# A four-layer transformer on one core: norms of keys and queries as products that accumulate into the feature banks

## The reference, cut to what matters

```python
def _apply_kernel(x, orf):                      # orf: 64 x 16
    m, d_k = orf.shape
    proj = jnp.einsum('bhld,md->bhlm', x, orf) / d_k ** 0.25
    norm = jnp.sum(x * x, axis=-1, keepdims=True) / (2.0 * math.sqrt(d_k))
    return (jnp.exp(proj - norm) + EPS) / math.sqrt(m)
...
q_phi, k_phi = _apply_kernel(q, orf), _apply_kernel(k, orf)
kv = jnp.einsum('bhlm,bhld->bhmd', k_phi, v)
ksum = jnp.sum(k_phi, axis=2)
num = jnp.einsum('bhlm,bhmd->bhld', q_phi, kv)
den = jnp.einsum('bhlm,bhm->bhl', q_phi, ksum)
out = num / den[..., None]
```

## Time and profile before

| | |
|---|---|
| median of 3 runs | 4754.18 us (4749.86 to 4757.36) |
| the profiled execution, its own time | 4758.76 us |
| its span, first to last instruction | 4757.0 us |
| mean granted TensorE clock over the span | 0.954 of full |
| PE busy | 4457.9 us (94%) |
| DVE / ACT / POOL busy | 3497.9 / 2808.7 / 1012.3 us |
| first product of the FFN that follows the first attention | at 795.4 us |

### The profile page before, as it was taken

The page is one execution under the profiler, slowest core; times in us unless marked ns, Lnnn a source line. Parts: engine busy times, 40 slices in busy tenths (PEclk is TensorE's granted clock), DMA queues, the critical chain, the costliest instruction groups (busy, mean ns, idle before and its releaser), DMA issues.

```text
span 4757.0 us, 66155 instructions
## 1 busy us (share of the span) xinstructions
PE 4457.9 (94%) x25753; PEld 1669.5 (35%) x25756; DVE 3497.9 (74%) x3850; ACT 2808.7 (59%) x5305; POOL 1012.3 (21%) x990
## 2 busy tenths in 40 slices
PE   8888888999997999999999999999999999999886
PEld 5444444666662222222222222222222232222285
DVE  3443447887887778888777888777888988888432
ACT  3222232333333778888777777777777757787721
POOL 2333335344422110000211111112111011100213
PEclk9888889999997999999999999999999999999998
DMA  3001000012212421211333221223222221222232
GB/s 103 25 29 58 19 19 11 10 49 77 71 71 67 128 79 67 69 48 62 121 97 106 73 76 68 83 95 122 71 80 75 63 70 45 87 67 79 72 116 54
DMA packets 230533, 330.73 MB, mean 70 GB/s; under 512 B 37030, under 2 KB 171752, under 8 KB 228168
## 3 DMA queue, kind: packets, MB, share of 16 engines
q1 hardware_dynamic: 227340, 318.63, 20.3%
q0 software_dynamic: 2880, 7.87, 0.8%
HBM read 218.95 MB, written 98.04 MB: 67 GB/s over the span
## 4 chain that ended last, share of the span: by engine, by line
PE 69%; DVE 10%; DMA 3%; POOL 2%; issue 2%; ACT 1%; SPq 1%; POOLq 0%; DVEq 0%; another core or an unknown queue 0%; ACTq 0%
PE ps L751 68%; DVE mx L1630 4%; PE ps L754 2%; DMA pk<-Ob 1%; DVE stat L1454 1%; DVE hn L1448 1%; DVE hn L1609 0%; DMA rd<-pk 0%; DVE hn L1604 0%; SPq L2117 0%; DMA KS<-kd 0%; DVE eb L1465 0%; DMA QS<-mrow 0%; ACT Pb L1376 0%; DVE hs L1440 0%
## 5 line engine op out<-in xcount | busy, mean ns | idle before, releaser
L1630 DVE TENSOR_REDUCE mx<-ps 128x1 f32<-128x1024 f32 x2048 | 2407.3, 1219 | 449.9 <-PE ps L751 446.7
L1376 ACT ACTIVATE Pb<-ps 128x512 f32<-128x512 f32 x4096 | 2202.6, 597 | 533.1 <-PE ps L751 529.0
L751 PE MATMUL ps<-QS,KS 98*128 98x512 bf16 x4096 | 1255.4, 387 | 16.5 <-ACT Pb L1376 7.7
L751 PE MATMUL ps<-Pb,VA 128*32 128x512 f32 x8192 | 1105.0, 612 | 0.1
L751 PE MATMUL ps<-KM,QM 64*128 64x512 bf16 x4096 | 661.1, 390 | 47.3 <-DVE mx L1630 45.7
L751 PEld LDWEIGHTS ps<-QS,KS 98*128 98x128 bf16 x4096 | 260.1, 98 | 1100.1 <-ACT Pb L1376 908.3
L751 PEld LDWEIGHTS ps<-KM,QM 64*128 64x128 bf16 x4096 | 179.3, 93 | 605.1 <-issue 357.0
L751 PEld LDWEIGHTS ps<-Pb,VA 128*32 128x32 f32 x8192 | 161.8, 108 | 403.2 <-issue 402.2
L1944 POOL CAST mrow<-mres 16x128 bf16<-16x128 f32 x64 | 18.1, 283 | 1293.2 <-ACT mres L1198 1293.2
L1502 DVE TENSOR_TENSOR phi<-ps,ns 128x1024 f32<-128x1024 f32 x64 | 78.2, 1222 | 188.6 <-PE ps L751 188.4
L751 PE MATMUL ps<-wdT,hT 128*128 128x256 f32 (+1 forms) x768 | 194.3, 396 | 15.5 <-DVE X L1615 14.1
(11 more groups left out here) (255 smaller groups left out, 4500.9 us busy)
## 6 DMA issues: line engine op xcount, KB each, us to landing
QM<-qd SPq DMA_DIRECT2D x128, 256.0 KB
KM<-kd SPq DMA_DIRECT2D x128, 256.0 KB
qd<-parts SPq DMA_DIRECT2D x96, 256.0 KB, 2.7
kd<-parts SPq DMA_DIRECT2D x96, 256.0 KB, 2.8
QS<-qd SPq DMA_DIRECT2D x64, 384.0 KB
KS<-kd SPq DMA_DIRECT2D x64, 384.0 KB
vdr<-vst SPq DMA_DIRECT2D x64, 256.0 KB, 2.5
den<-rd SPq DMA_DIRECT2D x64, 256.0 KB
```

The costliest lines, as they stand in the source:

```text
L751: return eng.matmul(out, a, b, start=start, stop=stop, skip_group_check=skip)
L1376: eng.activation(Pb[(u - 1) % 9], o, ACT.Exp, bias=0.0, scale=0.25).then_inc(act_A, 1)
L1630: eng.tensor_reduce(mx4[qc % 2][:, 4 * i + q, h:h + 1], o, AX, ALU.max).then_inc(dve_D, 1)
```

## The change

The norms are no longer a result of their own. A block matrix `Nblk` (128 x 512, laid out as `Wblk` is, each block filled with -0.125) is loaded, and the squares `k2` and `q2` are multiplied with it on the same row tiles as `kT` and `qT` are with `Wblk`, accumulating into the same banks. ACT takes the exponential of the keys from the banks (before: DVE added, ACT worked from `phi`). The steps `kn` and `nq`, DVE's addition and its four splitting instructions, `n8`, `nq`, `selq` and their transfers and POOL's conversion go. The plan's rules are rewritten in smaller pieces: `o` and `q` steps are split, and key steps stand between most query steps.

```diff
 def keys_order(b):
-    made = lambda C: [("k", C, 0), ("k", C, 1), ("v", C, 0), ("v", C, 1), ("kn", C)]
+    made = lambda C: [("k", C, 0), ("k", C, 1), ("v", C, 0), ("v", C, 1)]
...
 def queries_order(b, chunks, way):
...
-        for ht in range(2):
-            yield [("q", C, ht)]
-        yield [("fq", C), ("nq", C)]
-        for ht in range(2):
-            for g in range(2):
-                yield [("pq", C, ht, g)]
-            yield [("num", C, ht)] + ([("res", C)] if ht else [("ap0", stats)] if stats is not None else [])
+        yield [("q", C, 0)]
+        yield [("q", C, 1), ("fq", C)]
+        for ht, g in ((0, 0), (0, 1), (1, 0)):
+            yield [("pq", C, ht, g)]
+        yield [("num", C, 0)] + ([("ap0", stats)] if stats is not None else [])
+        yield [("pq", C, 1, 1)]
+        yield [("num", C, 1), ("res", C)]
...
-    behind = {"q": (0, 2), "nq": (2,), "pq": (0, 1, 0, 1), "num": (0, 2), "o": (0, 1)}
+    behind = {"q": (1, 2), "pq": (1, 1, 1, 2), "num": (0, 3), "o": (1, 0)}
...
         def phi_(n):
             w.wait_ge(act_k, at["k", C, 1])
+            w.wait_ge(pool_k2, at["k", C, 1])
             w.wait_ge(dve_setup, 4)
+            w.wait_ge(ld_n, 16)
             if n:
-                w.wait_ge(dve_phi, n)
+                w.wait_ge(act_phi, n)
             for ht in range(2):
-                for r in range(2):
-                    s = slice(64 * r, 64 * r + 64)
-                    d = mm(bank(1 + r)[:, 256 * ht:256 * ht + 256], kT[C % 2][s, ht, j * P:(j + 1) * P], Wblk[s, 256 * r:256 * r + 256])
+                for x, wt_ in ((kT, Wblk), (k2, Nblk)):
+                    for r in range(2):
+                        s = slice(64 * r, 64 * r + 64)
+                        d = mm(bank(1 + r)[:, 256 * ht:256 * ht + 256], x[C % 2][s, ht, j * P:(j + 1) * P], wt_[s, 256 * r:256 * r + 256],
+                               x is kT, x is k2)
...
         def pq(C, ht, g):
+            w.wait_ge(pool_q, at["q", C, 1])
             for k in range(2):
                 s, c = slice(32 * (2 * g + k), 32 * (2 * g + k) + 32), slice(P * (2 * g + k), P * (2 * g + k) + P)
                 mm(bank(b5 + k), Wblk[s, c], qT[i][s, ht, :], True, False)
-            w.wait_ge(dve_nq, 3 * at["nq", C])
-            w.wait_ge(pool_setup, 6)
             for k in range(2):
-                d = mm(bank(b5 + k), selq[0:96, 4 * ht + 2 * g + k, :], way_of(C)["stk"][0:96, :], False, True)
+                s, c = slice(32 * (2 * g + k), 32 * (2 * g + k) + 32), slice(P * (2 * g + k), P * (2 * g + k) + P)
+                d = mm(bank(b5 + k), Nblk[s, c], way_of(C)["q2"][s, ht, :], False, True)
...
         def phi_(n):
-            w.wait_ge(dve_phi, n + 1)
-            eng.activation(phi[n % 3], phi[n % 3], ACT.Exp, bias=0.0, scale=1.0).then_inc(act_phi, 1)
+            w.wait_ge(pe_phi, n + 1)
+            if n > 2:
+                w.wait_ge(pe_kv, n - 2)
+            eng.activation(phi[n % 3], bank(1, 2), ACT.Exp, bias=0.0, scale=1.0).then_inc(act_phi, 1)
...
-            w.wait_ge(ld_selq, 16)
-            eng.tensor_copy(flat(selq[0:96]), flat(phq[0][0:96, 0:2, :])).then_inc(pool_setup, 1)
...
-            load(n8, t["n8"]).then_inc(ld_n, 16)
-            load(flat(nq), t["nq"]).then_inc(ld_n, 16)
+            load(Nblk, t["nb"]).then_inc(ld_n, 16)
...
-            load(flat(phq[0][0:96, 0:2, :]), t["selq"]).then_inc(ld_selq, 16)
```

More of the change, by code:

```diff
@@ L49, in keys_order @@
             n = 4 * C + j
-            yield [("phi", n)] + [("kv", n - 2)] * (n % 16 > 1)
+            yield [("phi", n)]
+            if n % 16 > 1:
+                yield [("kv", n - 2)]
             if ahead:
-                yield ahead[j:j + 1] if j < 3 else ahead[3:]
+                yield ahead[j:j + 1]
         if b == 0:
@@ L516, in program @@
     Wblk = take("Wblk", [P, 512])
-    n8 = take("n8", [P, 8])
-    nq = take("nq", [P, 2, 96])
-    selq = take("selq", [P, 8, P], BF16)
+    Nblk = take("Nblk", [P, 512])
     kvS = take("kvS", [P, 256])
@@ L527, in program @@
     va = [take(f"va{i}", [P, 4, 16, 32]) for i in range(2)]
-    ns = [take(f"ns{i}", [P, 4, 16]) for i in range(2)]
     phi = [take(f"phi{i}", [P, 1024]) for i in range(3)]
@@ L760, in k @@
             if C < 4:
[L761 to L764, removed]
+                if C:
+                    w.wait_ge(act_k, at["k", C - 1, ht])
             elif ht:
@@ L866, in q @@
             else:
-                w.wait_ge(act_kn, 4)
+                w.wait_ge(act_k, at["k", 3, 1])
             mm(bank(b4), WT["q"][:, 0, ht * P:(ht + 1) * P], xq_[i][:, 0, :], True, False)
             mm(bank(b4), WT["q"][:, 1, ht * P:(ht + 1) * P], xq_[i][:, 1, :], False, True).then_inc(pe_q, 1)
[L871 to L877, removed]
         def pq(C, ht, g):
@@ L889, in pq @@
             else:
-                w.wait_ge(dve_phi, 64 if C else 0)
+                w.wait_ge(act_phi, 64 if C else 0)
+            w.wait_ge(pool_q, at["q", C, 1])
             for k in range(2):
@@ L1264, in q @@
             eng.activation(qT[C % 2][:, ht, :], bank(b4), ACT.Identity, bias=bqk["q"][:, ht:ht + 1], scale=1.0).then_inc(act_q, 1)
-        def nq_(C):
-            b4 = way_of(C)["banks"][0]
-            w.wait_ge(pe_nq, at["nq", C])
-            if former(C) is not None:
-                w.wait_ge(pe_num, at["num", former(C), 1])
-            else:
-                w.wait_ge(pe_kv, 64 if C else 0)
-            copy(way_of(C)["stk"][0:96, :], bank(b4)[0:96, :]).then_inc(act_nq, 1)
         def pq(C, ht, g):
@@ L1494, in bo @@
             eng.tensor_tensor(bvo["o"], bank(7)[:, 0:256], bvo["o"], ALU.add).then_inc(dve_setup, 1)
-        def phi_(n):
-            C, j = divmod(n, 4)
-            w.wait_ge(pe_phi, n + 1)
-            w.wait_ge(act_kn, C + 1)
-            if n > 2:
-                w.wait_ge(pe_kv, n - 2)
-            eng.tensor_tensor(phi[n % 3].rearrange("p (a b) -> p a b", a=16), bank(1, 2).rearrange("p (a b) -> p a b", a=16),
-                              wide(ns[C % 2][:, j, :], 16, 64), ALU.add).then_inc(dve_phi, 1)
         def kvt(b):
@@ L1813, in yn @@
             norm_apply(xr[g][:, 5 * f:5 * f + 5, :], ("yp", g, f), 5)
-        stages = {"setup": setup, "wq": wq, "wb": wb, "bo": bo, "phi": phi_, "kvt": kvt, "nq": nq_, "num": num, "o": o, "st0": st0,
+        stages = {"setup": setup, "wq": wq, "wb": wb, "bo": bo, "kvt": kvt, "num": num, "o": o, "st0": st0,
                   "ap0": ap0, "fold": fold, "qx": qx, "up": up, "qa": qa, "qb": qb, "qc": qc, "da": da, "st1": st1,
@@ L1841, in k @@
             w.wait_ge(act_k, at["k", C, ht])
-            w.wait_ge(pe_kn, C - 1 if C > 1 else 0)
+            if C > 1:
+                w.wait_ge(pe_phi, 4 * (C - 1))
             x = kT[C % 2][:, ht, :]
@@ L1852, in q @@
             if former(C) is not None:
-                w.wait_ge(pe_nq, at["nq", former(C)])
+                w.wait_ge(pe_pq, at["pq", former(C), 1, 1])
             else:
-                w.wait_ge(pe_kn, 16 if C else 0)
+                w.wait_ge(pe_phi, 64 if C else 0)
             x = qT[C % 2][:, ht, :]
@@ L2251, in layout @@
     a["wo2"] = f(np.asarray(inputs["L1_ffn_wo"]).reshape(8, 8, P, D).transpose(0, 2, 1, 3).reshape(8, P, 2048))
-    n8, nq, sq = np.zeros((P, 8), np.float32), np.zeros((P, 2, 96), np.float32), np.zeros((96, 8, 2, 64), np.float32)
+    nb = np.zeros((P, 512), np.float32)
     for h in range(8):
-        n8[16 * h:16 * h + 16, h] = -0.125
-        for i in range(3):
-            for k in range(2):
-                nq[16 * h:16 * h + 16, k, 32 * i + 8 * k + h] = -0.125
-                sq[32 * i + 8 * k + h, 4 * k + h // 2, h % 2] = 1.0
-    a["n8"], a["nq"], a["selq"] = n8, nq.reshape(P, 192), sq.reshape(96, 1024)
+        nb[16 * h:16 * h + 16, 64 * h:64 * h + 64] = -0.125
+    a["nb"] = nb
     a["ident"] = np.eye(P, dtype=np.float32)
```

67 lines of the change are left out of this document (18 added, 49 removed).

## The result

The changed kernel takes 4640.6 us (median of 4, 4639.7 to 4647.3) against 4753.6 for the kernel before (4 runs): 0.9759 of its time, 95% interval 0.9736 to 0.9783, 113 us less. The forecast was 4690, the range 4655 to 4735: right in direction, 49 us short, and outside the range. Rival (b) had named 4645. The profiled execution of the changed kernel has a span of 4637.7 us, 119.3 less.

The account below looks back on a forecast made before the run. The first attention was taken as bound by PE, by its work, waits and clock. Keys alone -1, idle time -49, work +19, clock -34 and last batch 0 sum to -65 us, giving 4690; range 4655 to 4735.

Parts of the forecast that it names:

- Rival (b): Clock full nearly always, since PE idles less: -111 us, 4645; chance 0.12.
- The clock: Middle stretch of the first attention: time at 1.2 GHz falls from 194 to 110 us, worth -34 us.
- Work and idle time of the middle: Middle stretch: PE's added less removed products cost +19 us; PE's idle time falls from 91 to 41, -49 us.
- The step prices: PE's steps at full clock in the changed kernel: `phi` 1.95 us, `pq` 1.94 us.
- the fixed part: The 0.19 us of a `phi` step not due to its products, taken as paid once when products double.
- rival (c): Cost eats the gain: fixed part paid twice, idle 60 instead of 41, half the clock gain; -5 us, 4750; chance 0.09.
- the wait of `q`: Middle stretch: `q`, right behind the second `o`, waits 0.75 us for DVE's addition, 12 times, 9 us.
- Keys alone: Opening stretch with keys only: earlier start and clock gain against added products, sum -1 us.
- Last batch: Final stretch without keys: fewer waits against six `pq` steps perhaps at half clock; 0 us, bounds -12 and +10.
- (a): Clock stays as it is while the waits go: -31 us, 4725; chance 0.20.
- (d): Slower: `pq` steps on 32-row tiles repeatedly pull the clock down; at 350 us of half clock +33, 4787; chance 0.07.

Follow-up runs that it names:

- run 11: Changed kernel with the last batch's steps in the old order and the `ap0` right ahead of `kvt` put behind it; 4627.3 us, ratio 0.9750.
- run 9: Changed kernel with one key step moved, so nothing stands between the first two `pq` steps of a chunk; 4667.5 us, ratio 0.9807.
- run 1: Changed kernel's products in the step order of the kernel before, less `kn` and `nq`; 4726.5 us, ratio 0.9913.
- run 5: Changed kernel with the eight 8-column products of `kn` added again per chunk of keys, without a wait; 4685.8 us, ratio 0.9874.
- run 8: Run 1 with key steps moved to stand between the two `pq` steps of each half; 4645.1 us, ratio 0.9772.
- run 3: Kernel before with only the keys' norms changed (no `kn`), queries and order as before; 4710.9 us, ratio 0.9880.
- run 2: Kernel before, its norms (`kn`, `nq`) kept, in the change's new order; 4744.0 us, ratio 0.9964.
- run 10: Kernel before with POOL's conversion of the selector moved behind the squares of the second chunk; 4751.4 us in one run.

## Why the prediction was wrong

**The clock is the term that failed.** The prediction let the time at half clock fall from 194 to 110 us, "one stretch of 9 us per chunk", for the place `pq`, `kv`, wait, `pq`. It fell to 23. The price of a microsecond at half clock was nearly right: the busy time of PE in the kernels with the new products, 448 us with 10 at half (run 11), 477 with 71 (run 9), 506 with 138 (run 1), rises by 0.45 to 0.47 for each, where the sum had 0.91 x 0.45 = 0.41. So the term is (195 - 23) x 0.45 = -77 instead of -34, and these 43 us, 36 by the amount and 7 by the price, are most of the 54 by which the profiled sum missed (119 against 65). What was mis-sized is how much stays at the place that was left alone. It kept its wait of 0.5 us, and by the clock records not one stretch at 1.2 GHz begins there. Four begin in the middle of the changed kernel, all in or behind waits of 2.6 to 4.6 us: one for `aT`, one for the reciprocal and two for `kvD`, the wait that was not seen ahead. A wait of 0.5 us between two `pq` steps hardly counts in these traces, one of 1.1 does (run 9). The causes that the prediction named are the right ones: the narrow products of `kn` (run 5, +58 us at half clock) and the long waits behind `pq` (run 8, -109). With one of them left, much stays: 94 us without `kn` (run 3), 143 with the new order (run 2, with its new wait).

**Work and idle time of the middle were right.** Extrapolated to full clock by 0.45, PE's work is 444 us in the changed kernel and 427 to 432 in the kernel before and in run 2: +12 to +17, forecast +19. The step prices are as forecast, so the fixed part is paid once (part of rival (c) falls). Idle time is 41.7, forecast 41, and a part of that agreement is luck: the wait of `q` came as forecast (8.3 for 9), but the wait for the sums' copy (8.6) was missed, and of the unexplained rest less was left.

**Keys alone**: -2.6, forecast -1. The first `phi` came 6.9 us earlier as forecast, and run 10, with 5.6 of them by moving POOL's conversion and nothing else, shows the main cause; `kn` (1.8) stands ahead of `phi` there still.

**Last batch**: +8.7, forecast 0 within -12 and +10. The reason given for a loss does not hold as stated. The windows of the changed kernel over the first and the second row of six `pq` steps:

```profile
594.40:604.70 10.30, 10.30 (x48) 4.32 (x48) 0.00 (x0) 6.41 (x7) 5.70 (x6) 1.00 0.22 80
640.20:653.40 13.20, 13.18 (x40) 5.98 (x40) 0.00 (x0) 4.11 (x5) 4.00 (x4) 0.52 0.01 1
```

The first runs at 2.4 GHz throughout; the second begins at 1.2 GHz, behind a wait of 3.79 us for POOL's squares, and stays there until 653.0 by the clock records, 12.7 us of such products. It then comes back to 2.4 GHz while they still run: the pair at 653.44 takes 0.96 us again. So 10 us of products on 32 rows did not pull the clock down here, and once it was down it stayed so for 12.7 us of them. In the whole last batch the time at 1.2 GHz rose from 14 us to 41. There is also a wait of 11 us for `aT`, for which the last section has the cause; the timeline of PE has it as

```profile
678.32 3.78 PE L744 MATMUL ps<-WoT,aT 128*128 128x256 f32 x8 [11.05 <-DVE aT L1486]
```

and the one in the kernel before at that place was 1.2 us.

**The rivals.** (a) would have kept 194 us at half clock, and (d) would have raised them; both fall with the 23. (b) came true in its number, and its reason only half: the Trainium skill (TensorE: Matmul & The Clock Gate, What's actually happening) has activity release the throttle, by how busy PE has been. Less idle time did go with a higher clock, but run 5 has less idle time than the changed kernel (33 against 42) and three and a half times the time at half clock. Busy time as the profile counts it does not explain that alone, and what of a narrow product counts instead these runs do not settle.

**Behind the first attention** the changed kernel's trace is 15 us shorter (3961.6 to 3946.5), in code that no kernel here changed. The clock is in it: the time at 1.2 GHz in that part fell from 220 us to 189, which at 0.45 is 14 us, and PE's busy time there fell by 16. Over the profiles of all fourteen kernels this part lies between 3939.5 and 3967.2 us and its time at 1.2 GHz between 175 and 220, and the two rise together by 0.48 us for each. Why the clock differs there from kernel to kernel is open, and that the change caused the 15 us was not shown: run 10, whose one edit lies at the very start, differs there from the kernel before as well (210 against 220, 3959.5 against 3961.6).

## What to carry to other kernels

Price a wait of TensorE in a stage whose granted clock is mixed at more than its length: here 8 us more of waiting, in 12 waits of 1.1 us between two `pq` steps, cost 31 us. Two causes of a low clock, of which one was enough to keep much of it, gave most of their gain only when both were gone. Look for steps with very narrow products (8 columns here); they cost work, and clock behind them, and here more products in their place were the cheaper choice. When rules of order are rewritten for the steady state, check the ends of batches and the last stretch separately: two small edits there took 25 us more off the profiled span (4637.7 to 4612.3), and 13 off the median.

## What the runs showed of the hardware

Gains from a higher clock did not add. In the middle stretch the products alone gave 32 us and the order alone 36 (with a new wait of 22 us in it), both 110; the time at 1.2 GHz fell by 56, 51 and 171 us.

DVE's plain operations in SBUF can wait for POOL's. Four layer-norm instructions of DVE take 8.64 us in the last batch of the changed kernel, where 56 of them take 33.3 us of busy time in all, 0.65 mean. The timeline of DVE and of POOL there:

```profile
665.90 8.64 DVE L1429 TENSOR_SCALAR X<-X,mv,rstd 128x256 f32<-128x256 f32 x4
674.46 3.35 DVE L1481 RECIPROCAL rB<-ps 128x512 f32<-128x512 f32 x1
```

```profile
664.90 4.72 POOL L1780 TENSOR_TENSOR X<-X,bo 128x1024 f32<-128x1024 f32 x2
669.59 2.38 POOL L1864 TENSOR_TENSOR fq<-fq,fc 128x1024 f32<-128x1024 f32 x1
672.05 2.34 POOL L1866 TENSOR_TENSOR fq<-fc,fq 128x1024 f32<-128x1024 f32 x1
```

They end when POOL's run of additions ends (674.4), and the reciprocal behind them, whose `aT` the step `o` waits for, is late: the four layer-norm instructions ahead, at 660.55, took 1.37 us together. The Trainium skill (SBUF — State Buffer, Terms) has DVE and GpSimd hold a shared pair of ports for a whole instruction. The trace agrees: one by one the four take 1.53, 2.42, 2.43 and 2.50 us, each until the addition of POOL beside it ends, while the 36 of the 56 with no work of POOL beside them take 0.40 to 0.41. In run 11, where the last batch has the order of before, the same four come before POOL's additions start:

```profile
641.09 2.21 DVE L1437 TENSOR_SCALAR X<-X,mv,rstd 128x256 f32<-128x256 f32 x4
```

```profile
645.47 4.69 POOL L1788 TENSOR_TENSOR X<-X,bo 128x1024 f32<-128x1024 f32 x2
```

There the wait of PE for `aT` at that place is 0.18 us instead of 11.05. The order of the steps around it differs too, so not all of the 11 us belong to the ports.
